# Four triangle layers on one core: the transposed picture between layers 1 and 2 kept in three gapless blocks and gathered tile pair by tile pair, and layer 0's last variance taken from whole squares

## The reference, cut to what matters

```
x = x + L0(gn(x));  x = x + L1(gn(x));  x = x + L2(gn(x));  x = x + L3(gn(x))

# a layer, on xn = layernorm(gn(x)) (layer 3: gn(x) itself)
left, right = (xn @ Wl) * sigmoid(xn @ Wlg), (xn @ Wr) * sigmoid(xn @ Wrg)
out[i, j] = sum_k left[i, k] * right[j, k]      # layers 0 and 1, per channel
out[i, j] = sum_k left[k, j] * right[k, i]      # layers 2 and 3
result = (layernorm(out) * sigmoid(xn @ Wog)) @ Wout
```

## Time and profile before

| | |
|---|---|
| median of 3 runs | 1529.07 us (1520.78 to 1530.68) |
| the profiled execution, own time | 1531.67 us |
| its span in the profile | 1529.5 us |
| mean granted TensorE clock | 0.948 |
| PE, DVE, ACT, POOL busy | 84%, 68%, 63%, 36% |
| DMA | 249.31 MB in 206501 packets, 53.1% of 16 engines' span |

### The profile page before, as it was taken

The page is one execution under the profiler, slowest core; times in us unless marked ns, Lnnn a source line. Parts: engine busy times, 40 slices in busy tenths (PEclk is TensorE's granted clock), DMA queues, the critical chain, the costliest instruction groups (busy, mean ns, idle before and its releaser), DMA issues. The chain is left out here.

```text
span 1529.5 us, 43851 instructions
## 1 busy us (share of the span) xinstructions
PE 1282.1 (84%) x12950; PEld 765.9 (50%) x12950; DVE 1041.8 (68%) x2976; ACT 962.0 (63%) x2093; POOL 543.4 (36%) x490
## 2 busy tenths in 40 slices
PE   0899998787789998989941999999789677799898
PEld 0455554444345455755521666667455333367455
DVE  7577774299789996219950788831499788821587
ACT  0577774489577774129940888831599688822575
POOL 0455551055456563005530666610156200000355
PEclk9899999899899999999975899999899899999999
DMA  8011113467533332896667333359689444369798
GB/s 275 27 52 46 51 51 111 114 202 225 169 101 103 106 115 72 254 286 177 195 152 188 103 115 113 108 174 300 180 262 278 154 141 138 129 185 307 212 291 258
DMA packets 206501, 249.31 MB, mean 163 GB/s; under 512 B 29024, under 2 KB 196320, under 8 KB 206432
## 3 DMA queue, kind: packets, MB, share of 16 engines
q1 hardware_dynamic: 206432, 248.42, 53.1%
HBM read 139.83 MB, written 108.53 MB: 162 GB/s over the span
## 5 line engine op out<-in xcount | busy, mean ns | idle before, releaser
L989 DVE SCALAR_TENSOR_TENSOR lr<-ps,mask,act_out 128x128 f32 (+5 forms) x1152 | 276.3, 310 | 61.7 <-ACT act_out L739 55.6
L1153 POOL TENSOR_TENSOR rstd<-ve,half_col 128x6 f32<-128x6 f32 x144 | 190.2, 1321 | 259.1 <-DVE ve L962 225.4
L511 PE MATMUL ps<-w_parts,val 64*128 64x256 bf16 (+1 forms) x2112 | 222.6, 304 | 47.4 <-DVE lr L989 41.9
L1196 POOL TENSOR_TENSOR new_ring<-val,lr 128x384 f32<-128x384 f32 x96 | 103.4, 1078 | 409.5 <-issue 325.0
L1186 POOL TENSOR_TENSOR val<-act_out,gate_ring 128x384 f32<-128x384 f32 x96 | 118.4, 1233 | 247.2 <-ACT act_out L817 231.1
L739 ACT ACTIVATE act_out<-ps 128x384 f32<-128x384 f32 x384 | 174.9, 481 | 34.2 <-PE ps L511 16.7
L783 ACT ACTIVATE in_ring<-ps 128x768 f32<-128x768 f32 (+1 forms) x64 | 51.8, 810 | 184.0 <-PE ps L579 161.9
L511 PEld LDWEIGHTS ps<-w_parts,val 64*128 64x128 bf16 (+1 forms) x2112 | 90.5, 111 | 133.3 <-DVE lr L989 94.7
L1085 DVE TENSOR_TENSOR sq_low<-sq 128x384 bf16<-128x384 f32 x192 | 120.1, 625 | 52.9 <-ACT sq L796 52.8
L621 PE MATMUL ps<-in_ring,k 128*128 128x384 f32 x288 | 134.5, 555 | 20.1 <-DMA in_ring<-t_scratch 19.7
L715 ACT ACTIVATE cen<-ps,gn 128x384 f32<-128x384 f32 x144 | 83.6, 581 | 104.1 <-PE ps L466 101.5
(11 more groups left out here) (101 smaller groups left out, 2574.8 us busy)
## 6 DMA issues: line engine op xcount, KB each, us to landing
gate_scratch<-gate_ring SPq DMA_DIRECT2D x192, 192.0 KB, 2.2
gate_ring<-gate_scratch SPq DMA_DIRECT2D x96, 384.0 KB, 3.7
in_ring<-x_scratch SPq DMA_DIRECT2D x144, 192.0 KB, 2.4
lr<-x_scratch SPq DMA_DIRECT2D x72, 384.0 KB, 4.5
in_ring<-t_scratch SPq DMA_DIRECT2D x144, 192.0 KB, 3.3
x_scratch<-new_ring SPq DMA_DIRECT2D x48, 384.0 KB, 2.9
t_scratch<-in_ring SPq DMA_DIRECT2D x48, 384.0 KB, 3.4
lr<-x SPq DMA_DIRECT2D x6, 1536.0 KB, 15.3
```

The costliest lines, as they stand in the source:

```text
L511: mm = nc.tensor.matmul(banks[h][:, :, 0:P], moving(x, s)[half(h), N * r:N * r + P], proj_weights(w, h)[:, 0:2 * P], start=start, stop=sto ...
L989: ins = nc.vector.scalar_tensor_tensor(out5[:, h, lo // 2:hi // 2, :, m], ps[:, 4 + 2 * r + h, lo:hi].rearrange("p (a e) -> p a e", e=2), ...
L1153: nc.gpsimd.tensor_tensor(rstd[:, s % 2, :], ve[:, s % 2, :], half_col[:, :], ALU.pow)\
```

## The change

The transposed picture is written by ACT into three blocks of `lr` with nothing between their elements: tiles 0 to 23, 24 to 39 and 40 to 47 (`TURN_CUTS`). A block is stored as it lies to a DRAM tensor of its own (`turned_scratch0` to `2`): the first in 4 shares and the second in 4, among layer 1's last tiles (`step_and_store`), the third after the last tile. Layer 2's first phase fills a pair of slots by `gather`: 12 DMAs, for 3 blocks, 2 halves of channels and 2 halves of rows, each 64 partitions x 4 rows x 48, 32 or 16 positions. `keep` then stores the pair, which is now in natural order, to `x_scratch`, and a slot pair may be filled again only when its `keep` has landed (`natural_stored`). With the natural order, `x_parts` and `column_parts` go: one matmul and one `finish` per tile in layer 2. Apart from this, in layer 0's last phase `square_low` is left out and the variance is 3 float32 matmuls on the whole square.

```diff
@@ -54,6 +53,9 @@
 GATE_FIRST = (True, False, True, False)
+TURN_CUTS = (0, 24, 40, TILES)
+SHARES = 4
+QUARTERS = 4 * (len(TURN_CUTS) - 1)
 RES_SLOT = (None, 48, 32, 32)
...
@@ -61,6 +63,8 @@
     gate_dram = nc.dram_tensor("gate_scratch", [TILES, P, TILE], F32).ap()
+    turned_dram = [nc.dram_tensor(f"turned_scratch{q}", [P, N, ROWS * (b - a)], F32).ap()
+                   for q, (a, b) in enumerate(zip(TURN_CUTS, TURN_CUTS[1:]))]
     t_f32 = nc.dram_tensor("t_scratch", [C, N * N], F32).ap()
...
@@ -178,7 +182,10 @@
-turned = lr[:, 0:N * HALF].rearrange("p (j i) -> p j i", i=HALF)
+def turned(q):
+    first, behind = ROWS * TURN_CUTS[q], ROWS * TURN_CUTS[q + 1]
+    return lr[:, N * first:N * behind].rearrange("p (j i) -> p j i", i=behind - first)
...
@@ -189,18 +196,6 @@
     return t_dram(l).rearrange("c (h t f) -> h c t f", h=2, f=TILE)[:, :, bass.ds(n, 2), :]
-def column_parts(l, tile):
-    if l != 2:
-        return [tile]
-    return [tile.rearrange("p (r h i) -> p h r i", h=2, r=ROWS)[:, h, :, :] for h in range(2)]
-def x_parts(l, tile):
-    if l != 2:
-        return [tile]
-    return [tile.rearrange("p (h r i) -> p h r i", h=2, r=ROWS)[:, h, :, :] for h in range(2)]
...
@@ -257,16 +252,22 @@
-def over_tiles(eng, step, reach=RING):
+def over_tiles(eng, step, reach=RING, cut=None, later=None):
     last = TURNS - reach // RING
     for s in range(RING):
         step(s, 0, s, TILES - 1 - s)
-    with eng.Fori(1, last) as i:
+    if cut:
+        with eng.Fori(1, cut) as i:
+            for s in range(RING):
+                step(i * RING + s, i, s, reach)
+        for n in range(cut * RING, (cut + 1) * RING):
+            step(n, cut, n % RING, TILES - 1 - n)
+    with eng.Fori(cut + 1 if cut else 1, last) as i:
         for s in range(RING):
-            step(i * RING + s, i, s, reach)
+            (later or step)(i * RING + s, i, s, reach)
     for n in range(last * RING, TILES):
...
@@ -303,6 +304,34 @@
+        def gather(n, s):
+            for q in range(len(TURN_CUTS) - 1):
+                for h in range(2):
+                    for h2 in range(2):
+                        rows = bass.ds(HALF * h2 + ROWS * n, 2 * ROWS)
+                        columns = slice(HALF * h + ROWS * TURN_CUTS[q], HALF * h + ROWS * TURN_CUTS[q + 1])
+                        slot = in_ring[C * h2:C * h2 + C, s:s + 2, :].rearrange("p a (r i) -> p (a r) i", r=ROWS)
+                        sp.dma_start(slot[:, :, columns], turned_dram[q][C * h:C * h + C, rows, :])\
+                            .then_inc(in_loaded[s], 16)
+        def keep(n, i, s):
+            sp.wait_ge(in_loaded[s], in_count(l) + 16 * QUARTERS * (i + 1))
+            sp.dma_start(two_tiles(scratch, n), in_ring[:, s:s + 2, :]).then_inc(natural_stored[s // 2], 16)
+        def step_gathering(n, i, s, ahead):
+            if s % 2 and ahead >= RING + lead - 1:
+                sp.wait_ge(used, l * TILES + n + lead + 1)
+                sp.wait_ge(natural_stored[s // 2], 16 * (i + 2))
+                gather(n + lead + RING - 1, s - 1)
+            sp.wait_ge(a_gate, l * TILES + n + 1)
+            sp.dma_start(gate_dram[n, :, :], gate_ring[:, s, :]).then_inc(gate_stored[s], 16)
+            if s % 2 and ahead >= RING + 1:
+                keep(n + RING + 1, i + (s + 5) // RING, (s + 1) % RING)
         def step(n, i, s, ahead):
...
@@ -312,6 +341,18 @@
+        if l == 2:
+            for n in range(0, RING, 2):
+                gather(n, n)
+            for n in range(0, RING, 2):
+                keep(n, 0, n)
+            for n in range(0, RING, 2):
+                sp.wait_ge(used, l * TILES + n + 2)
+                sp.wait_ge(natural_stored[n // 2], 16)
+                gather(RING + n, n)
+            keep(RING, 1, 0)
+            over_tiles(sp, step_gathering, 2 * RING)
+            return
         if l:
...
@@ -331,6 +372,9 @@
                     .then_inc(planes_stored[g % 2], 16)
+            if l == 2 and g == 0:
+                for pair in range(PAIRS):
+                    sp.wait_ge(natural_stored[pair], 16 * TURNS)
             for n in freed_slots(l, g) if l else []:
...
@@ -383,21 +427,35 @@
-        over_tiles(sp, step, 2 * RING)
+        def store_turned(q, share, shares):
+            rows = slice(N // shares * share, N // shares * (share + 1))
+            sp.dma_start(turned_dram[q][:, rows, :], turned(q)[:, rows, :]).then_inc(turned_stored, 16)
+        def step_and_store(n, i, s, ahead):
+            step(n, i, s, ahead)
+            if s == RING - 1 and n < TURN_CUTS[2]:
+                sp.wait_ge(b2_turned, TURN_CUTS[1])
+                store_turned(0, i - TURN_CUTS[1] // RING, SHARES)
+            elif s == RING - 1:
+                sp.wait_ge(b2_turned, TURN_CUTS[2])
+                for half in range(2):
+                    store_turned(1, 2 * (i - TURN_CUTS[2] // RING) + half, SHARES)
+        if l != 1:
+            over_tiles(sp, step, 2 * RING)
         if l == 1:
+            for n in range(RING):
+                step(n, 0, n, TILES - 1 - n)
+            with sp.Fori(1, TURN_CUTS[1] // RING) as i:
+                for s in range(RING):
+                    step(i * RING + s, i, s, 2 * RING)
+            for n in range(TURN_CUTS[1], TILES):
+                step_and_store(n, n // RING, n % RING, TILES - 1 - n)
             sp.wait_ge(b2_turned, TILES)
-            quarters = scratch.rearrange("t (h2 c) (h f) -> h h2 c t f", h2=2, h=2)
-            for part, tiles in enumerate((slice(0, EARLY), slice(EARLY, TILES))):
-                for h in range(2):
-                    for h2 in range(2):
-                        rows = turned[C * h:C * h + C, h2 * HALF:(h2 + 1) * HALF, :]
-                        sp.dma_start(quarters[h, h2, :, tiles, :],
-                                     rows.rearrange("p (t r) i -> p t (r i)", r=ROWS)[:, tiles, :])\
-                            .then_inc(turned_stored[part], 16)
-            sp.wait_ge(turned_stored[0], 16 * 4)
+            store_turned(2, 0, 1)
+            sp.wait_ge(turned_stored, 16 * (2 * SHARES + 1))
         else:
...
@@ -622,8 +681,15 @@
         def variance(n, s):
-            pe.wait_ge(b2_sq_lo, base + n + 1)
             slot_free(pe, b2_std, base + n - 1)
+            if l == 0:
+                pe.wait_ge(b2_sq, base + n + 1)
+                for j in range(CHUNKS):
+                    mm = nc.tensor.matmul(ps[:, 6 + s % 2, 2 * j:2 * j + 2],
+                                          sq[:, s % 2, P * j:P * j + P], k_sel, start=True, stop=True)
+                mm.then_inc(b2_var, 1)
+                return
+            pe.wait_ge(b2_sq_lo, base - TILES + n + 1)
             for j in range(CHUNKS):
...
@@ -818,14 +884,19 @@
-        def turn(n, s):
+        def turn(n, s, q):
             act.wait_ge(b2_new, base + n + 1)
-            nc.scalar.activation(turned[:, :, bass.ds(ROWS * n, ROWS)].rearrange("p j i -> p i j"),
+            at = ROWS * n - ROWS * TURN_CUTS[q]
+            nc.scalar.activation(turned(q)[:, :, bass.ds(at, ROWS)].rearrange("p j i -> p i j"),
                                  new_ring[:, s, :].rearrange("p (r j) -> p r j", r=ROWS),
                                  ACT.Copy).then_inc(b2_turned, 1)
-        def step(n, i, s, ahead):
+        def block_of(n):
+            return sum(n >= cut for cut in TURN_CUTS[1:-1])
+        def step(n, i, s, ahead, q=0):
             if ahead >= 2:
...
@@ -1060,13 +1133,10 @@
-                res = x_parts(l, residual_slot(l, n))
                 slot_free(dve, new_stored[s // 2], 16 * (l // 2 * TURNS + i))
-                for new, out, x in zip(column_parts(l, new_ring[:, s, :]),
-                                         column_parts(l, ps[:, 4 + s % 2, 0:TILE]), res):
-                    ins = nc.vector.scalar_tensor_tensor(new, out, bias, x, ALU.add, ALU.add)
-                ins.then_inc(b2_new, 1)
+                nc.vector.scalar_tensor_tensor(new_ring[:, s, :], ps[:, 4 + s % 2, 0:TILE], bias, residual_slot(l, n),
+                                               ALU.add, ALU.add).then_inc(b2_new, 1)
             else:
...
@@ -1086,7 +1156,7 @@
         def step(n, i, s, ahead):
-            if ahead >= 4:
+            if l and ahead >= 4:
                 square_low(n + 4, s)
...
```

More of the change, by code:

```diff
@@ L38 @@
 PIECES = 6
-EARLY = 8
 SUBS = ROWS * TILES
@@ L146, in build_triangle_layers @@
         consts_loaded, params_loaded = sem("consts_loaded"), sem("params_loaded")
-        turned_stored = sems("turned_stored", 2)
+        turned_stored, natural_stored = sem("turned_stored"), sems("natural_stored", PAIRS)
         consts_ready, shift_ready, bias_mm, params_chain, params_ready = (
@@ L235, in plane_out, with in_count @@
             return main.rearrange("p (d q) -> p d q", q=N), tail.rearrange("p (d q) -> p d q", q=N)
-        def in_count(l):
-            return 16 * TURNS * (l - 1)
+        def in_count(l, s=0):
+            return 16 * TURNS * ((l > 1) + (l > 2) * (QUARTERS if s % 2 == 0 else 0))
```

(35 more changed lines are left out.)

## The result

| | before | after |
|---|---|---|
| median of 4 runs each, on one chip | 1527.34 us | 1616.4 us (1612.23 to 1620.11) |
| ratio after/before, 95% interval | | 1.0589 [1.0555, 1.0623] |
| span of the profiled execution | 1529.5 us | 1610.0 us |
| granted clock of TensorE, mean | 0.948 | 0.931 |

The account below looks back on a forecast made before the run. SP's queue was to bound layer 2's first phase. 1531.67 us + 77.5 (handover and that phase) + 4 (layer 1) + 0 (layer 0) - 4 (layer 2's last phase) = 1609 us, 5% slower; range 1550 to 1665.

Parts of the forecast that it names:

- What bounds the phase: Layer 2's first phase: SP's queue becomes the bound, 12.0 us a pair where PE and DVE need 6.76.
- In the loop 12.0 us a pair: Layer 2's first phase: 12 gathers at 0.71, gate store 0.4, keep's landing 2.9, semaphores 0.2 us.
- The stretch ahead of the loop: Layer 2's first phase: first gathers, keeps and two unrolled cycles of 10.8 us, to 57.6 us before the 18 loop cycles.
- The handover: Between layers 1 and 2: gives back some 27 us of idle PE, all and more lost in the 20 cycles.
- PE replaces DVE as the bound; 0 us: Layer 0's last phase: DVE relieved, PE slowed by float32 matmuls to 2.08 to 2.29 us a tile; ends -9 and +6.
- below 85%: Layer 0's last phase: sign that the forecast is right, DVE busy below 85% with PE above 90%.
- Layer 2's last phase, "-4": One finish instruction instead of two saves 0.13 us a tile, with PE near; -4 us, ends -6 and 0.
- Layer 1, "+4": Layer 1's last phase: stores of blocks 1 and 2 run beside it; +4 us, ends 0 and +12.
- The engines and the pieces: Rival in layer 2's first phase: gather traffic of 10.4 us a pair binds; 1647 us, chance 0.17 with the half clock.
- The half clock: Rival in layer 2's first phase: PE stays at half speed, two tiles about 12.8 us; chance 0.17 shared with the engines.
- the cheap short gathers: Rival on SP's queue: a gather costs 0.44 us in the loop, 0.47 ahead of it; 1539 us, chance 0.11.
- The queue keeps up: Rival in layer 2's first phase: SP's work on a pair stays under 6.76 us, compute binds; 1496 us, chance 0.08.

Follow-up runs that it names:

- e2: Changed kernel with blocks laid out in DRAM for six gathers of 128 partitions a pair, same pieces, each share's store split in two; 1494.26 us, ratio 0.9780.
- e3: Changed kernel with the keep store of a pair issued after the first four gathers of the next pair; 1591.98 us, ratio 1.0399.
- e4: Changed kernel without the keep stores and the waits for them, layer 2's residual read from layer 0's picture; 1575.91 us, one run.
- e8: e6 with layer 2's finish split into two instructions of 192 columns, as in the kernel before; 1495.38 us, ratio 0.9784.
- e6: Changed kernel with six gathers of 128 partitions a pair and the keep store issued after the first two of them; 1490.01 us, ratio 0.9745.
- e1: Changed kernel with each gather fetching two of its four rows, same number of DMAs, half of the pieces; 1615.94 us, ratio 1.0574.

## Why the prediction was right, and where its sizes were off

**What bounds the phase: right.** The forecast made SP's queue the bound, with twelve issues a pair and a stand at `natural_stored`, and the signs that it named for this phase are there: issues of 0.599 us (0.61 forecast), one gap a pair of 2.34 us between the keep's issue and the next gather (2.5), with one gate store in it, gathers that PE waits for. PE has half of its records in the window, though it is busy for 66% of it (99 of 150 us, at a granted clock of 0.77) and not for half. e2, e3 and e4 are the proof: fewer issues with the same pieces, the keep moved, and no keep, each take away what their share of the cycle says.

**"In the loop 12.0 us a pair": too small, 12.95.** This step is the one that failed in size. The landing of the keep was right (2.9 forecast from its issue, 2.73), and so was the issue itself. The register work between two issues was taken as 0.10 us, by a row of plane loads; it is 0.77 - 0.60 = 0.17. That is 0.8 us a pair. From the last gather to the keep it is 0.94 us where 0.4 and 0.2 for semaphores stood, 0.3 more, and the landing gave 0.2 back. 18 cycles of 0.95 more are 17 us. The stretch ahead of the loop gave 5 more (849.88 - 787.43 = 62.4 us, forecast 57.6): the first 24 gathers were right (15.79 against 15.1), but the second 24 took 17.06, and the two unrolled cycles 11.7 and 12.3 instead of 10.8. What follows the last cycle was about 3 us shorter than forecast, which brings the sum to 19. The last block's store (780.2 to 787.43, 7.2 us, against 7.3) was right.

**The handover: right.** The last `turn` to PE's start was 49.0 us and is 797.13 - 780.2 = 16.9, so 32 us of idle time come back (27 forecast), all given up again in the twenty cycles.

**Layer 0's last phase, "PE replaces DVE as the bound; 0 us": -7.6.** DVE is no longer the bound, as forecast, but the bound is ACT and not PE. The window from 320 to 380 us in after, away from both ends of the phase:

```profile
320.00:380.00 60.00, 59.57 (x378) 44.82 (x378) 52.07 (x125) 60.00 (x157) 31.23 (x32) 1.00 0.85 254
```

ACT is busy without a gap. PE has 59.57 us, but its weight loads wait for ACT's `rb` 20 times there. DVE has 87%, not the "below 85%" that was named as a sign. PE's rows in after, the six float32 records of one tile and what follows them:

```profile
331.04 0.73 PE L688 MATMUL ps<-k,sq 128*128 128x2 f32 x6
331.63 0.32 PE L680 MATMUL ps<-in_ring,centre_bf 128*128 128x384 bf16 x1
...
333.62 0.32 PE L680 MATMUL ps<-in_ring,centre_bf 128*128 128x384 bf16 x1
```

From the first record to the next matmul is 0.59 us, within the 0.54 to 0.75 of the forecast. What failed is the sum: it laid the records on PE's busy time of before, 1.70 us a tile, and made it 2.08 at the least. But DVE issues 125/4 = 31.2 tiles in the window, 1.92 us a tile, and PE needs no more than this. That is somewhat under the 1.98 that the forecast had taken as ACT's floor, from two instructions of one tile. From the first to the last `finish` it is 102.0 us before and 91.3 in after, 10.7 less; 3.1 us are lost again ahead of the first one (304.3 and 307.4 us). In that start PE also has matmuls whose results nothing uses (`keep_clock`), and from 300 to 320 us it is busy for 19.50 of 20 us (18.40 in before). There PE is the bound, and the longer records cost what the forecast feared: ACT waits for the variance for 8.6 us between 300 and 395 us, against 2.0 in before.

**Layer 2's last phase, "-4": -10.1.** `finish` was priced by its own duration, 0.13 us a tile and PE close behind. e8 against e6 shows 0.13 a tile; in after the first finish is at 1186.07 and the last at 1281.38, 95.3 us or 2.03 a tile, against 102.7 us before (1097.73 to 1200.42). So 7.4 of the 10.1 us lie in the phase itself. The other 2.7 us lie ahead of the first `finish`. e8 gives nearly all back (195.2 us for the stretch), 2 us of it in the same place beside e6, so both seem to come with the split; by what way it acts there was not settled.

**Layer 1, "+4": +2.1.** The stores were hidden, at a DMA share of 0.79 against 0.58. `turn` with short strides costs less than feared (median 998 ns against 1130).

**The rivals.** The engines and the pieces fell with e1. The half clock fell with e2, where the clock returns by itself once the gathers keep up; the cheap short gathers with the 0.599 us of after. "The queue keeps up" was not this kernel. Where the queue does keep up, in e2 and e6, the times are 1494 and 1490 against its 1496, but this nearness is partly luck: the sum lacks the 7.6 us of layer 0 and 6 of the 10.1 us of layer 2's last phase, and it does not have the 12.8 us by which e2's gathers start late. The Trainium skill's sentence that initiating is usually small relative to the DMA itself ("DMA: Bandwidth & Descriptors", "Issuing engines are not separate DMA queues") does not hold for this row: 0.60 of a gather's 2.2 us to landing is issue, and twelve of them follow each other.

## What to carry to other kernels

Count the DMAs that one step puts on a queue, price each by the row of the same partition count with the register work around it, and compare the sum with what a step of compute takes: a layout that saves one long transfer can lose more by making many short issues. Choose the layout in DRAM so that one DMA spans all 128 partitions. A store whose landing the same queue must await belongs amid other issues, not right ahead of the wait; that pays where the queue is the bound (24 us in e3) and hardly where it is not (4 us in e6, not clear of the noise). The same holds for the stores: a layout that widens the loads should not split the stores (12.8 us in e2). And a term for a new bound cannot be had by adding to an engine's busy time, if the engine was not the bound before.

## What the runs showed of the hardware

- Issuing a gather of 64 partitions took 0.599 us, one of 128 partitions with the same pieces for each partition 0.373 (e2): the wider DMA was the cheaper one to issue.
- Pieces of 64 to 192 bytes did not bind at this rate: half as many moved the DMA share from 0.37 to 0.27 and the time not at all (e1).
- Float32 matmuls with two columns and full weights took 0.59/6 = 0.10 us a record.
- Behind stores of a share as two DMAs of 64 partitions (e2), SP's plane loads of layer 1 took longer to issue than behind the single ones of after. From SP's timeline of e2, two plane loads behind a store:

```profile
739.35 1.13 SPq L439 DMA_DIRECT2D turned_scratch<-lr  x2
740.84 4.44 SPq L391 DMA_DIRECT2D in_ring<-t_scratch  x2
```

In after two such loads behind a store take 1.87 us at most (1.1 to 1.2 otherwise), and the last `turn` starts at 779.3 against 786.0 in e2. Why was not looked into.
